# Routing tokens to experts by gathers: a slot table inverted on TensorE, halves of x stored once, and u projected ahead of k and v

## What is computed

```python
xn = _layernorm(x)
# attention branch: 16 heads of 16, no softmax over the tokens
q = k = elu(heads(xn @ Wqk + bqk))
v = silu(xn @ Wv + bv);  u = silu(xn @ Wu + bu)
kv = einsum('bhnd,bhne->bhde', k, v)
a = u * layernorm(einsum('bhnd,bhde->bhne', q, kv), ln_g, ln_b)
# expert branch: 8 experts, the 2 best of each token
w, i = top_k(softmax(xn @ gate_w.T), 2);  w = w / w.sum()
y_e = (silu(xn @ w1[e].T) * (xn @ w3[e].T)) @ w2[e].T
out = x + a @ Wo + bo + sum over the token's two experts of w * y_e
```

## Time and profile before

| | before |
|---|---|
| median of 3 runs | 314.33 us (313.32 to 315.13) |
| profiled execution | 314.47 us |
| span of its profile | 312.7 us |
| TensorE matmuls busy | 238.6 us, 76% |
| VectorE | 182.6 us, 58% |
| ScalarE | 156.6 us, 50% |
| GpSimd | 149.5 us, 48% |
| mean granted TensorE clock | 0.931 of full speed |

### The profile page before, as it was taken

The page is one execution under the profiler, slowest core; times in us unless marked ns, Lnnn a source line. Parts: engine busy times, 40 slices in busy tenths (PEclk is TensorE's granted clock), DMA queues, the critical chain, the costliest instruction groups (busy, mean ns, idle before and its releaser), DMA issues.

```text
span 312.7 us, 5876 instructions
## 1 busy us (share of the span) xinstructions
PE 238.6 (76%) x1656; PEld 148.1 (47%) x1656; DVE 182.6 (58%) x433; ACT 156.6 (50%) x288; POOL 149.5 (48%) x128
## 2 busy tenths in 40 slices
PE   0328999598740049999999999997999998699820
PEld 0117456264540014566766666665666654355510
DVE  3897999988950004776859586775675232233300
ACT  2876956998770003537374545534464443244310
POOL 5374458888887700051431324424463435143561
PEclk9999899799976558999999999999999999999995
DMA  7999952559932244696876966899899899989663
GB/s 223 376 430 426 426 205 70 135 120 302 228 128 101 101 98 87 100 140 98 120 117 93 133 108 114 114 157 143 115 117 138 119 136 113 176 114 132 108 86 34
DMA packets 90001, 49.11 MB, mean 157 GB/s; under 512 B 78098, under 2 KB 87314, under 8 KB 88788
## 3 DMA queue, kind: packets, MB, share of 16 engines
q1 hardware_dynamic: 80020, 33.36, 50.9%
q0 software_dynamic: 9952, 15.38, 27.1%
HBM read 18.01 MB, written 15.38 MB: 107 GB/s over the span
## 4 chain that ended last, share of the span: by engine, by line
PE 46%; POOL 18%; DMA 14%; DVE 9%; issue 8%; POOLq 2%; SPq 0%; ACT 0%; DVEq 0%
PE bank L1114 28%; POOL slots L411 17%; PE bank L1127 12%; DMA regions<-slots 7%; PE bank L1165 3%; DMA out<-xrow 3%; DMA area<-x 3%; DVE kT L689 2%; POOLq L432 2%; PE bank L1142 1%; PE bank L1154 1%; DVE area L812 1%; DMA slots<-xrow,slot 1%; DVE wa L695 1%; DVE stats L677 1%
## 5 line engine op out<-in xcount | busy, mean ns | idle before, releaser
L1114 PE MATMUL bank<-regions 128*128 x468 | 110.1, 386 | 28.5 <-DMA regions<-slots 25.6
L441 POOL DMA_INDIRECT out<-xrow x39 | 63.0, 1616 | 117.2 <-issue 53.0
L1114 PEld LDWEIGHTS bank<-regions 128*128 128x128 f16 x468 | 44.9, 99 | 80.1 <-issue 35.1
L917 DVE SCALAR_TENSOR_TENSOR regions<-bank,regions 128x512 f32<-128x512 f32 x39 | 27.0, 692 | 68.0 <-PE bank L1114 65.7
L1127 PE MATMUL bank<-regions 128*128 x468 | 57.5, 273 | 3.4 <-DMA regions<-regions 3.4
L596 ACT ACTIVATE regions<-regions 128x512 f16<-128x512 f32 x39 | 24.6, 630 | 57.8 <-DVE regions L917 57.8
L1127 PEld LDWEIGHTS bank<-regions 128*128 128x128 f16 x468 | 45.4, 98 | 16.0 <-issue 5.4
L591 ACT ACTIVATE regions<-bank 128x512 f32<-128x512 f32 x39 | 23.3, 597 | 51.6 <-PE bank L1114 51.2
L411 POOL DMA_INDIRECT slots<-xrow,slot x32 | 41.2, 1287 | 12.8 <-issue 9.4
L922 DVE TENSOR_TENSOR regions<-regions 128x512 f16<-128x512 f32 x39 | 26.9, 690 | 21.6 <-ACT regions L596 21.6
L1035 PE MATMUL bank<-wa,xT 128*128 128x512 f16 x96 | 26.0, 412 | 0.0
(11 more groups left out here) (142 smaller groups left out, 293.5 us busy)
## 6 DMA issues: line engine op xcount, KB each, us to landing
regions<-wexp SPq DMA_DIRECT2D x8, 1536.0 KB, 21.9
out<-xT POOLq DMA_DIRECT2D x8, 256.0 KB, 8.5
area<-x SPq DMA_DIRECT2D x2, 768.0 KB, 7.8
regions<-wattn SPq DMA_DIRECT2D x1, 1032.0 KB, 10.7
out<-padrow POOLq DMA_DIRECT2D x1, 896.0 KB, 11.7
regions<-slots SPq DMA_TRANSPOSE x39, 3.3
regions<-regions SPq DMA_TRANSPOSE x39
xrow<-slots SPq DMA_DIRECT2D x39, 1.0 KB, 2.7
```

The source lines that it names most:

```text
L441: g.indirect_dma_start(out, bass.IndirectOffsetOnAxis(ap=meta[:, t, 0:1].bitcast(I32), axis=0), ysb[t % RING], None, compute_op=ALU.add).t ...
L917: v.scalar_tensor_tensor(h32[t % 2], ps_b[t % 2][:], 1.0 / SCALE, s32[t % 2], ALU.mult, ALU.mult).then_inc(h_ready, 1)
L1114: last = mm(bank_[:], xg[t % 4][:, KD * d + k, :], w16[:, bass.ds(e, 1), w, at:at + I].rearrange("p a c -> p (a c)"), start=(k == 0 and n ...
```

## The change

Tokens are no longer written to slots; each slot tile fetches its tokens.

- SP stores both halves of normalised x to DRAM in token order (`xsplit`), four tiles at a time, between the loads of expert weights (`store_split`).
- VectorE splits each slot number into a multiple of 128 and a rest, and compares both with counters: `hi_hot` (1248 elements) and `lo_hot` (4096). Three products of `hi_hot` carry token number and the gate's two halves (`rows16`, two on GpSimd, one on VectorE). TensorE multiplies the two, 32 matmuls (`invert`), and PSUM then holds the token and the gate of each slot. `row_tables` makes of them `row_in`, `row_out` and `row_gate`.
- GpSimd's `gather(t)` fetches 128 rows by `row_in`; `load_x(t)` turns them from SBUF to SBUF. `row_gate` and `row_out` take the place of `meta`.
- All of `u_proj` and `u_out` come before `qv(2)`; their PSUM banks are now two of those of `qv`.
- The experts' conversions 6 and 7 move into the loop's first tiles; the first scaling for expert 0 and all of `k_lo` move to GpSimd; k's halves have two buffers; the attention's pairs begin two tiles later, so that `add_attention` stands at tiles 17 and 29.

The diff, cut to its core; lines of before that are only removed are in the functions above.

```diff
-PAIR_AT = [2 + 3 * p for p in range(NP)]
+GATE_SCALE = 1024.0
+EARLY = 6
+AHEAD = 9
+PAIR_AT = [4 + 3 * p for p in range(NP)]
...
+        stage = sums16.bitcast(F32)
+        lo_hot = sums16[:, 0:TOPK * TT * P].rearrange("p (n c) -> p n c", c=P)
+        rows16 = sums16[:, TOPK * TT * P:TOPK * TT * (P + NV * ST)].rearrange("p (n v s) -> p n v s", v=NV, s=ST)
+        xg = [xg_all[:, r, :].rearrange("p (c i) -> p c i", i=P) for r in range(4)]
+        hi_hot = xg_all[:, :, :].rearrange("p r c -> p (r c)")[:, 0:TOPK * TT * ST].rearrange(
+            "p (n s) -> p n s", s=ST)
+        s32 = [view(stage, I * r, [I]) for r in range(2)]
+        xgr = [view(stage, I * 2 + D * r, [2 * D], F16) for r in range(4)]
...
-        ps_x, ps_u = ps_qv, bank[0:2]
+        ps_x, ps_u = ps_qv, bank[6:8]
...
-        slots = nc.dram_tensor("slots", [ST * P, ROW], F32, kind="Internal").ap()
+        xsplit = nc.dram_tensor("xsplit", [TOKENS, 2 * D], F16, kind="Internal").ap()
...
+                    sp.wait_ge(xl_dve, last - DVE_LO)
+                sp.dma_start(split_tiles[:, CH * c:last, :], xrow16[:, CH * c:last, :]).then_inc(split_stored, 16)
+            load_expert(0)
+            load_expert(1)
+            load_expert(2)
+            for c in range(TT // CH):
+                store_split(c)
+                load_expert(3 + c)
             sp.wait_ge(attn_lo, 1 + KD)
             load_expert(E - 1)
...
-            transpose_k(0)
-            transpose_k(1)
-            transpose_k(2)
...
-            for g in range(TT // CH):
...
-            sp.wait_ge(scattered2, 16 * TT)
-            sp.wait_ge(w_lo, E - 2)
...
             def load_x(t):
+                sp.wait_ge(gathered[t % 4], 16 * (t // 4 + 1))
...
+            pool.wait_ge(w_hi, 1)
+            part = regions[:, 2 * WCOLS:2 * WCOLS + POOL_COLS]
+            g.tensor_scalar(part, part, SCALE, None, ALU.mult).then_inc(w_scaled, 1)
...
+            pool.wait_ge(split_stored, 16 * (TT // CH))
+            pool.wait_ge(hi_hot_ready, 1)
+            for n, per_row in enumerate((token1[:], gates16[:, 0, :])):
+                g.tensor_tensor(rows16[:, :, n, :], hi_hot, per_row.unsqueeze(2).broadcast_to([P, TOPK * TT, ST]),
+                                ALU.mult).then_inc(rows_pool, 1)
...
+            g.dma_start(out[TOKENS:TOKENS + SPARE, :], x[0:SPARE, :]).then_inc(y_added[1], 16)
...
+            def gather(t):
+                wait(pool, xg_loaded[t % 4], 16 * (t // 4))
+                g.indirect_dma_start(xgr[t % 4], None, xsplit,
+                                     bass.IndirectOffsetOnAxis(ap=row_in[:, t:t + 1], axis=0)
+                                     ).then_inc(gathered[t % 4], 16)
+            def k_lo(i):
+                for r in range(CH):
+                    t = CH * i + r
+                    pool.wait_ge(kh_ready, 2 * (t + 1))
+                    g.tensor_tensor(krow[i % 2][:, r, D:2 * D], kv32[r][:, 0:D], krow[i % 2][:, r, 0:D],
+                                    ALU.subtract).then_inc(kl_ready, 1)
+            pool.wait_ge(row_in_ready, 1)
+            for t in range(4):
+                gather(t)
+            for i in range(TT // CH):
+                k_lo(i)
+            for t in range(4, AHEAD):
+                gather(t)
...
             for t in range(ST):
                 if t in FIN_AFTER:
                     add_attention(*FIN_AFTER[t], t)
+                if t + AHEAD < ST:
+                    gather(t + AHEAD)
                 add_expert(t)
...
             hi(0)
-            act.wait_ge(w_hi, 1)
-            part = raw(0)[:, 0:POOL_COLS]
-            a.activation(part, part, ACT.Copy, scale=SCALE).then_inc(w_scaled, 1)
...
-            exps(0)
+            exps(0, range(2))
+            u_out(0)
+            u_out(1)
             halves(0, range(2))
+            for p in range(2, NP):
+                u_out(p)
             act.wait_ge(w_lo_pool, 1)
             act.wait_ge(w_lo_0, 1)
             hi(2)
+            exps(0, range(2, CH))
             halves(0, range(2, CH))
-            u_out(0)
-            u_out(1)
             act.wait_ge(w_lo, 1)
             hi(3)
             exps(1)
+            halves(1)
             act.wait_ge(w_lo, 2)
             hi(4)
-            halves(1)
-            u_out(2)
-            u_out(3)
-            act.wait_ge(w_lo, 3)
-            hi(5)
             exps(2)
             halves(2)
             kv_halves(0)
-            act.wait_ge(w_lo, 4)
-            hi(6)
-            u_out(4)
-            u_out(5)
+            act.wait_ge(w_lo, 3)
+            hi(5)
             exps(3)
-            act.wait_ge(w_lo, 5)
-            hi(7)
             halves(3)
-            u_out(6)
-            u_out(7)
             a.activation(warm[:], log_scale[:], ACT.Silu).then_inc(warm_done, 1)
             kv_halves(1)
...
-            chain(v.tensor_scalar(ge1, gate2[:], SCALE, SCALE, ALU.mult, ALU.add))
-            chain(v.reciprocal(gap, ge1))
-            v.tensor_copy(xrow[:, :, D + 1:D + 2], gap.unsqueeze(2)).then_inc(gate_ready, 1)
-            v.tensor_tensor(gate2[:], gate2[:], gap, ALU.mult).then_inc(gate_ready, 1)
+            chain(v.tensor_scalar(ge1, gate2[:], 1.0 / GATE_SCALE, 1.0 / GATE_SCALE, ALU.mult, ALU.add))
+            chain(v.reciprocal(gates[:, 0, :], ge1))
+            chain(v.tensor_tensor(gates[:, 1, :], gate2[:], gates[:, 0, :], ALU.mult))
+            gates_all = gates[:, :, :].rearrange("p k t -> p (k t)")
+            chain(v.tensor_copy(gates16[:, 0, :], gates_all))
+            chain(v.tensor_tensor(gates16[:, 1, :], gates_all, gates16[:, 0, :], ALU.subtract), first_expert_rest)
...
+            chain(v.tensor_copy(slot[:], slotf), k_map, 0)
+            chain(v.tensor_scalar(slot[:], slot[:], P - 1, None, ALU.bitwise_and), v_map, 0)
+            v.tensor_copy(slot_lo[:], slot[:]).then_inc(slot_ready, 1)
+            dve.wait_ge(slot_ready, 1)
+            chain(v.scalar_tensor_tensor(slot_hi[:], slot_lo[:], -1.0, slotf, ALU.mult, ALU.add), k_map, 1)
+            def per_row(u):
+                return u.unsqueeze(2).broadcast_to([P, TOPK * TT, ST])
+            v.tensor_tensor(hi_hot, per_row(slot_hi[:]), tile128[:].unsqueeze(1).broadcast_to([P, TOPK * TT, ST]),
+                            ALU.is_equal).then_inc(hi_hot_ready, 1)
+            dve.wait_ge(split_stored, 16 * (TT // CH))
+            v.tensor_tensor(lo_hot, slot_lo[:].unsqueeze(2).broadcast_to([P, TOPK * TT, P]),
+                            col_no[:].unsqueeze(1).broadcast_to([P, TOPK * TT, P]), ALU.is_equal
+                            ).then_inc(lo_hot_ready, 1)
+            dve.wait_ge(hi_hot_ready, 1)
+            v.tensor_tensor(rows16[:, :, 2, :], hi_hot, per_row(gates16[:, 1, :]), ALU.mult
+                            ).then_inc(rows_dve, 1)
+            v_map(1)
+            chain(v.tensor_tensor(end, base, tiles, ALU.add))
...
+            def row_tables():
+                dve.wait_ge(rows_done, 1)
+                token = ps_rows[:, 0:ST]
+                v.tensor_scalar(row_in[:], token, -1.0, 0.0, ALU.add, ALU.max).then_inc(row_in_ready, 1)
+                chain(v.scalar_tensor_tensor(is_pad, token, 0.0, spare1[:, 0:ST], ALU.is_equal, ALU.mult))
+                v.scalar_tensor_tensor(row_out[:], token, -1.0, is_pad, ALU.add, ALU.add).then_inc(row_out_ready, 1)
+                chain(v.tensor_copy(row_gate[:], ps_rows[:, ST:2 * ST]))
+                chain(v.tensor_tensor(row_gate[:], row_gate[:], ps_rows[:, 2 * ST:3 * ST], ALU.add))
+                v.tensor_scalar(row_gate[:], row_gate[:], 1.0 / (GATE_SCALE * SCALE), None, ALU.mult
+                                ).then_inc(row_gate_ready, 1)
+            row_tables()
...
-            v_map(3)
+            def some_maps(tiles):
+                for t in tiles:
+                    k_map(t)
+                    v_map(t)
+            some_maps(range(2, CH))
             expert_lo(1)
-            k_lo(0)
+            some_maps(range(CH, 2 * CH))
             expert_lo(2)
-            kv_maps(1)
+            some_maps(range(2 * CH, 3 * CH))
+            kv_blocks(0)
             expert_lo(3)
-            k_lo(1)
-            for c in range(3):
-                second_gates(c)
+            kv_lo(0)
+            some_maps(range(3 * CH, 4 * CH))
             expert_lo(4)
-            kv_maps(2)
-            second_gates(3)
-            kv_blocks(0)
-            expert_lo(5)
-            k_lo(2)
-            kv_lo(0)
-            expert_lo(6)
-            kv_maps(3)
-            expert_lo(7)
-            k_lo(3)
             kv_blocks(1)
             kv_lo(1)
+            expert_lo(5)
...
+                if t < E - EARLY:
+                    expert_lo(EARLY + t)
...
-            u_proj(0)
-            qv(CH)
-            qv(CH + 1)
-            u_proj(1)
...
+            def invert():
+                pe.wait_ge(lo_hot_ready, 1)
+                pe.wait_ge(rows_dve, 1)
+                pe.wait_ge(rows_pool, 2)
+                for n in range(TOPK * TT):
```

(17 more changed lines are left out.)

251 lines of the change are left out of this document (109 added, 142 removed).

## The result

The changed kernel took 319.34 us (median of 4 runs, 317.73 to 321.14) against 313.82 for the kernel before: ratio 1.0227, 95% interval 1.0175 to 1.028. It is slower by 2.3%, where the forecast was 311.2 us. The profiled execution took 317.73 us for a span of 315.9, so it is the fastest of the four. A median is of all executions of a kernel; the ratios leave out those that were over 1.5% slower than its fastest.

What follows compares the result with a forecast made beforehand. Bounds: scatters hold 22 us of the front, TensorE paces the loop at 4.73 us a tile. Span 312.7 - 9.1 + 1.0 + 5.0 = 309.6; with 1.77 around it and against the median, 311.2 us; own range 308 to 314, overall 303.5 to 319.

Steps and rivals of the forecast that it cites:

- D: Row tables to first expert matmul: groups 9.3 us apart, start at 104.7 instead of 113.78, 9.1 us gained.
- E: Filling the loop: conversions and a late k transposition hold up the first tiles; 1.0 us lost.
- F: Loop's end on GpSimd's queue: adds behind gathers that wait for x loads, later attention stop; 5.0 us lost.
- A: Front, up to slot numbers: scaling on GpSimd (1.6 us) delays VectorE's mask; slot numbers at 44.6 instead of 40.6.
- B: One-hots in the front: `lo_hot` 4.5 us, GpSimd's product 2.6, VectorE's 1.4; `v_map(1)` ends at 56.3.
- C: Front's loop through four engines: `invert` waits behind `u_proj`, which needs `v_map(1)`; TensorE idle 12 us, `rows_done` at 71.4.
- rival 2: Front's groups of four tiles each 1.2 us slower through `k_lo` on GpSimd: no change, 314.7 us; chance 0.18.
- rival 3: GpSimd's queue becomes the loop's bound from 3.9 us a tile: 316 us there, 319.5 at 4.2; chance 0.20.
- Rival 1: Engines do not hold each other up before and in the one-hots: 7.1 us less, 304.1 us; chance 0.20.
- this ring: Front's loop through four engines, from `v_map(1)` over `u_out` and `u_proj` to `invert`; TensorE idle for 12 us.

## Why the prediction was wrong

The sum was 309.6 for the span, and 315.9 came: 6.3 us more, about 2.1 from D, 1.2 from E and 3.1 from F. Step by step:

**A, the slot numbers**: 44.6 forecast, the last step ahead of the CAST ended at 45.7, and the mask at 40.7 instead of 39.3. The mechanism was the one described, and the traces of two runs confirm it. Its size was off: the scaling took 4.11 us on GpSimd and not 1.6. I had both bounds (1.48 and 3.18) from rows, and the value lay above both.

**B and C**: `v_map(1)` ended at 56.8 (56.3 forecast), the second half of `u_proj` began at 58.33 (57.8), `invert` ended at 70.9 (71.4). The total is right, but two errors within it cancel: GpSimd's product ran beside `lo_hot` instead of behind it, took 6.32 us instead of 2.6, and VectorE's product took 3.53 instead of 1.4. That 56.8 came out so near 56.3 was luck. `lo_hot` at 4.42 and `hi_hot` at 1.45 are at the rate taken: 1.08 and 1.16 ns an element, and L723 in the earlier trace rows has 1.09. The Trainium skill (VectorE: DVE Perf Modes, What auto-detection actually checks) gives an operation of two inputs the doubled rate only if every tensor is 16-bit with a step of 1 or -1; the trace agrees, with these 1.08 and 1.16.

**D**: the first expert matmul at 106.8 instead of 104.7; 7.0 us gained of the forecast 9.1. From `rows_done` on it took 35.9 instead of 33.3, and 0.5 of this was made good ahead of it. The groups stand 9.9 and 10.2 apart and not 9.3, which is 1.5, the first 0.3 less; from `exps(3)` at 100.01 to the first expert matmul it took 6.8 and not 5.35, another 1.45. ScalarE's timeline, the first `exps` of each group:

```profile
79.92 0.47 ACT L551 ACTIVATE area<-bank,log_scale 128x256 f32<-128x256 f32 x1
...
89.86 0.46 ACT L551 ACTIVATE area<-bank,log_scale 128x256 f32<-128x256 f32 x1
...
100.01 0.46 ACT L551 ACTIVATE area<-bank,log_scale 128x256 f32<-128x256 f32 x1
```

VectorE's conversions took up to 3.8 us beside `k_lo` on GpSimd, against 3.35, and `k_lo` itself 1.4 a tile there, against 0.7. This lies between the forecast and rival 2's mark of 10.5.

**E**: at tile 4 TensorE was 4.8 us ahead (126.78, and 131.58 in the timeline of the kernel before) and no longer 7.0, so filling the loop cost 2.2 and not 1.0.

**F is the step that failed.** The sum puts the last add at 305.0 - 9.1 + 1.0 + 5.0 = 301.9 (the prediction writes "about 301"), and it was issued at 308.27: 6.4 late, 2.1 of it from D, 1.2 from E, and 3.1 here. Add 28 was forecast at 265.5 on the clock before, hence 257.4 on the changed kernel's, and came at 267.90, 10.5 us late; the stop and the adds behind it then went faster than I had charged. The step treated the queue as one that follows TensorE at a fixed distance, and put the larger part of the loss on the stop's place at tile 29. The shift alone, in the kernel before, cost nothing that can be told from zero (1.0035). What there is in its place is **rival 3**: the gather makes the queue 3.96 us a tile, from the first stop on it is overfull, and the rival had its own mark, tile 29's add more than 27 us behind the hidden matmuls of tile 31. These end at 256.1, and the add is issued at 285.07: 28.9 us. Rival 3 gave 316 at 3.9 us a tile and 1.1 more for each 0.1; at 3.96 that is 316.7, and 317.73 was measured in the profiled execution, 319.34 in the median. It had a chance of 0.20. Its account of the lag was too mild as well: it had the queue 15 us behind after the first stop and level again at tile 28, and tile 17 was added 21.5 us after it was written, tile 28 still 14.0. About 6 of the 21.5 were there ahead of the stop, 7.4 to 11.8 where the kernel before has 2.0 to 4.4, since gathers wait for x loads. The run with the add ahead of the gather brought this down to 2.5 to 6.4, but its stop began no earlier, so it doesn't price this part.

The number that should have raised it stood in my own working. Behind the second stop the queue of before was full, and eleven adds took 32.8 us, 2.98 each with changes of expert. With a gather of 1.3 that makes 4.28 a tile, above the 3.9 from which the rival decides. It was too high for the 3.96 that came, but on the right side of 3.9. I used 3.45, from the bare durations of an add and a gather and a small share for the changes. Where a queue has slack, the waits at changes of expert lie inside its idle time and look free; between the stops of the kernel before, adds stood 3.50 us apart (twelve from 214.37 to 252.89), and a gather with its gap of 1.3 raised that by 0.46, so, as I read it, part of the gather went into idle time and the rest did not.

**The other rivals.** Rival 1 (no mutual blocking) is refuted by the 3.23 and 3.06 us operations. Rival 2's slower groups were there at half their size. By the Trainium skill (SBUF — State Buffer, Who interferes with whom) `tensor_tensor`, a VectorE operation of two inputs, is inferred not to hold up descriptor generation. No gather here stands beside a long `tensor_tensor`; beside another operation of two inputs the trace differs from what the prediction drew from the page: the gather at 109.36 took 3.90 us while L755 ran from 108.60, the next one, with VectorE idle of such work, 0.95.

The whole, then: the scatters stood for 22 us in the front; the gathers took their place in the loop, on the same queue, and that queue already carried two stops near its limit. That gathers and stops together make the loss is shown, by the two runs that leave out one or the other and by the two counter-tests of the stop's place. It reaches the end by two paths, the queue's own adds and TensorE's wait for a late gather, and which is longer changes from run to run. How the 0.46 us a tile splits between gaps, changes of expert and waits for landing is only read from the trace. A version that keeps the gathers and is faster than both exists: `v_map(1)` ahead of the comparisons and the scaling on ScalarE, 309.44 us against 312.32 for the kernel before beside it, ratio 0.9855. It does so by starting the loop 12 us earlier than the changed kernel; its queue is as full as before. How to relieve the queue itself, beyond leaving work out, stays open.

## What to carry to other kernels

Cost a queue from a stretch in which it is full, not from the bare durations of its instructions: there the waits for its own transfers are visible, and work added to it is hardly covered (here 4.28 us a tile by that sum, 3.96 measured, 3.45 by the durations). Compare that rate with the engine that sets the pace before calling added instructions covered, above all if the queue also has stops, since a full queue doesn't regain them. And look for a short operation on which several engines wait in a ring: here moving one of 0.41 us was worth 9.5, as much as the whole gain forecast for the front; the forecast had named this ring and priced it, and taken it as given. The chain that ended last shows one of several nearly equal chains; an edit that cuts it may give nothing.

## What the hardware showed that was not expected

- VectorE operations of 16 to 128 elements took 3.06 to 3.23 us, where their like take 0.2 to 0.3, while GpSimd's scaling or subtraction ran. It also happens while GpSimd reads one input only (L819 beside L426). It was one operation each time; the three behind L819 ran at 0.3 us while the scaling went on.
- The same GpSimd product of 1248 half-precision elements took 6.32 us, mostly beside `lo_hot`, and 3.49 when only its first 1.35 us fell beside VectorE's product, which itself took 3.53 where a comparison of that size alone took 1.45.
- The wait for the attention additions to land grew with their number: 6 to 10 us behind four, 10.9 behind eight of 256 KB.
